# Moving the feed-forward pairs of a two-pass software pipeline: first pairs at their last possible step, the later second pairs one step earlier

## What is computed

```python
x = x + 0.5 * _L1_ffn_ref(_layernorm(x), w_gate, w_up, w_down)      # first feed-forward
x = x + _L1_attn_ref(_layernorm(x), in_proj_weight, ...)           # second attention
x = x + 0.5 * _L1_ffn_ref(_layernorm(x), w_gate, w_up, w_down)      # second feed-forward
...
def fp4_linear(x, w):                      # blocks of 16 along the last dim
    return einsum(fp4_quant_dequant(x), fp4_quant_dequant(w))
gate = fp4_linear(x, w_gate); y = fp4_linear(x, w_up)
return fp4_linear(silu(gate) * y, w_down)  # 128 -> 352 -> 128
```

## Time and profile before

| | |
|---|---|
| median of 3 runs | 1892.03 us (1891.06 to 1893.39) |
| the profiled execution | 1895.74 us, its span 1893.7 us |
| the tail within the span | from about 1177 us to 1893.7 us |
| busy over the whole span | PE 84%, DVE 66%, ACT 54%, POOL 37% |
| granted clock of TensorE, by stretch | 0.77 (1177 to 1285 us), 0.92 (1285 to 1554), 1.00 (1554 to 1735), 0.84 (1735 to 1821), 0.62 (1821 to 1894) |
| PE busy in the same stretches | 64.2 of 108 us, 227.0 of 269, 149.6 of 181, 57.5 of 86, 34.6 of 73 |

### The profile page before, as it was taken

How to read it: one execution, slowest core, us unless ns; L and a number is a source line. 1 busy time by engine, 2 the same in 40 slices (tenths; PEclk the granted TensorE clock), 3 DMA queues, 4 the chain that set the end, 5 groups by cost and what they waited for, 6 DMA issues and landing times. The chain is left out here.

```text
span 1893.7 us, 35220 instructions
## 1 busy us (share of the span) xinstructions
PE 1583.6 (84%) x12162; PEld 1091.9 (58%) x12167; DVE 1250.6 (66%) x2566; ACT 1020.1 (54%) x2035; POOL 707.3 (37%) x1144
## 2 busy tenths in 40 slices
PE   6999947999999999998899993576888898878654
PEld 5668835555555555554666782354666676666443
DVE  6635558888888788882753665686668777675333
ACT  2434423788888888885333441233556656655421
POOL 0787634011111111111088763432344554443530
PEclk9999978999999999999699996688899999999876
DMA  6123421111111111110512343000000000000000
GB/s 246 36 78 85 133 69 31 34 29 34 29 29 40 29 34 29 29 29 8 201 47 84 95 119 108 3 1 1 2 2 2 8 5 7 5 7 8 4 7 8
DMA packets 50494, 83.08 MB, mean 44 GB/s; under 512 B 11124, under 2 KB 35124, under 8 KB 49652
## 3 DMA queue, kind: packets, MB, share of 16 engines
q1 hardware_dynamic: 41236, 62.07, 11.4%
q0 software_dynamic: 9088, 18.76, 2.9%
HBM read 43.18 MB, written 31.22 MB: 39 GB/s over the span
## 5 line engine op out<-in xcount | busy, mean ns | idle before, releaser
L1883 DVE TENSOR_REDUCE z_parts<-z_pM 128x4 f32<-128x512 f32 x576 | 373.2, 685 | 95.3 <-PE z_pM L1621 91.4
L1798 ACT ACTIVATE z_Pr<-z_pE 128x512 f32<-128x512 f32 x576 | 322.5, 597 | 84.9 <-PE z_pE L1645 82.1
L1990 POOL TENSOR_SCALAR_AFFINE_SELECT z_Pr<-z_Pr 128x512 f32<-128x512 f32 x128 | 81.6, 637 | 480.6 <-ACT z_Pr L1798 480.6
L1645 PE MATMUL z_pE<-z_QM,z_QK 128*128 128x512 f32 x576 | 250.5, 437 | 8.0 <-DMA z_QM<-z_Q 5.5
L1621 PE MATMUL z_pM<-z_KM,z_Q 128*128 128x512 f32 x576 | 233.5, 410 | 1.5 <-DVE z_Q L1873 0.9
L1645 PEld LDWEIGHTS z_pE<-z_QM,z_QK 128*128 128x128 f32 x576 | 107.6, 188 | 158.9 <-ACT z_Pr L1798 91.4
L356 POOL DMA_INDIRECT slot_results<-m_yq,m_xq x156 | 152.4, 977 | 74.8 <-ACT m_yq L561 43.1
L332 POOL DMA_INDIRECT slot_rows<-m_XN,m_dest x128 | 130.0, 1016 | 94.8 <-DVE m_dest L650 59.4
L1658 PE MATMUL z_pO<-z_Pr,z_V 128*9 128x512 f32 (+3 forms) x1536 | 159.3, 488 | 0.1
L960 PE MATMUL f_gup<-s_wguT,f_xT 128*128 128x352 f32 x256 | 117.5, 545 | 41.8 <-DVE f_src L1240 31.6
L1109 ACT ACTIVATE f_sg<-f_gup 128x176 f32<-128x176 f32 x128 | 40.7, 318 | 162.2 <-PE f_gup L960 162.0
(11 more groups left out here) (274 smaller groups left out, 3888.9 us busy)
## 6 DMA issues: line engine op xcount, KB each, us to landing
slot_rows<-in_c_pad SPq DMA_DIRECT2D x2, 5070.0 KB, 24.4
m_xq<-slot_rows SPq DMA_DIRECT2D x38, 260.0 KB, 3.5
z_QM<-z_Q SPq DMA_DIRECT2D x128, 64.0 KB, 2.0
z_KM<-z_QK SPq DMA_DIRECT2D x60, 128.0 KB, 2.4
m_raw<-in_gu SPq DMA_DIRECT2D x2, 2048.0 KB, 8.7
m_XN<-slot_results SPq DMA_DIRECT2D x8, 512.0 KB, 4.2
m_raw<-slot_results SPq DMA_DIRECT2D x8, 512.0 KB, 5.9
slot_results<-m_yq,m_xq POOLq DMA_INDIRECT x156
```

Source lines behind the costliest of these rows:

```text
L1645: mm(pE[e % 2][:, :].rearrange("p (h c) -> p h c", h=4), QK[G % RING][:, kt * P:(kt + 1) * P], QM[half][:, :, q * P:(q + 1) * P], start=Tr ...
L1798: a.activation(Pr[j % 4][:, :, q * P:(q + 1) * P], pE[e % 2][:, :].rearrange("p (h c) -> p h c", h=4), ACT.Exp, scale=DH0 ** -0.5).then_in ...
L1883: v.tensor_reduce(parts[:, qt, kb, :], pM[n % 3][:, :].rearrange("p (h k) -> p h k", h=4), AX.X, ALU.max).then_inc(maxed, 1)
L1990: g_.affine_select(blk, blk, [[0, 4], [1, P]], ALU.is_ge, 0.0, base=0, channel_multiplier=-1).then_inc(selected, 1)
```

## The change

Two table entries change. The first passes, which stood at steps 0 to 6 without a gap and then at every second step to 24, stand at 0, 1, 2, 4, 6, ... 28. The second passes, at 17, 19, ... 47, stand at 17, 19, ... 29 for pairs 0 to 6 and at 30, 32, ... 46 for pairs 7 to 15. The last step of all goes from 50 to 49. No instruction is added or removed but those that go with a quantisation of other width; the attention and the statistics keep their ticks.

```diff
     AHEAD = 12
-    FIRST = {p: p if p < 6 else 6 + 2 * (p - 6) for p in range(NP2)}
-    SECOND = {p: 2 * p + 17 for p in range(NP2)}
+    FIRST = {p: max(p, 2 * p - 2) for p in range(NP2)}
+    SECOND = {p: 2 * p + (17 if 2 * p + 16 <= FIRST[NP2 - 1] else 16) for p in range(NP2)}
     PAIR = {n: (p, 0) for p, n in FIRST.items()} | {n: (p, 1) for p, n in SECOND.items()}
```

## The result

The changed kernel takes 1874.8 us (median of 4 runs, 1874.29 to 1876.98), the kernel before 1892.7 us (1891.06 to 1895.32): ratio 0.9906, 95% interval 0.9889 to 0.9924, 17.9 us less. Timed again, with five runs of the changed kernel against 17 of the one before, it was 0.9903 (0.9889 to 0.9918). The forecast was 8.9 us less. So the direction and most of the places were right, but the gain was twice the forecast: 1874.8 us is inside the range of the prediction (1873 to 1892), near its low end, and outside the 1877 to 1888 of the forecast alone. A gain of more than 17 us, which came, had been given a chance of 0.05.

A forecast was written before the change was run, and what follows sets the result against it. PE work was taken to bound the tail's middle and a chain of Q and G halves its end. Terms from -12.6 to +6.3 us summed to -8.9, giving 1883.1 us; range 1873 to 1892, forecast alone 1877 to 1888.

The forecast's parts named there:

- a string of halves: Each pair's Q half (quantisation start, DVE L1216, to transposes, PE L952) and G half (to next L1216) sum to the end.
- The crowded ticks: Ticks 52 to 59 carry a first and a second pass per step: +6.3 us; 52 to 63 over 105 us means wrong.
- the step to pair 8: From tick 60 to second pair 8's quantisation, which starts two ticks earlier: -12.6 us.
- The stretch from pair 9 to 11: Halves beside full attention, sized from first passes in ticks 26 to 33: 60.4 us against 58.9, +1.5; low bound 56.
- the early ticks: Ticks 8 to 17, where steps 3 and 5 lose first passes: -1 us, bounds -10 and +4.
- pair 11's Q half: Still has scores and softmax beside it, so 12.2 us; pair 11 to 12 changes by 0.
- The end behind pair 15: Behind the start of the last second pair nothing changes: 0.
- The Q halves of pairs 12 to 14: Quantisation halves after the projections end: 9.1 us each, bounds 7.0 and 12.2.
- POOL's block: `inverse_root` and `expand` ahead of `scale_back` hold up the Q half; moved behind, 12.2 us becomes 9.1 in three halves.
- Q halves would not get shorter: Rival: statistics, added projection and attention on DVE replace POOL's work; 12.2 us stays, +9.3, 1892.4 us; chance 0.19.
- the scale comes too late: Rival: ACT's `normalise` waits for `inverse_root`; 1903 us if that takes 14; chance 0.13, shared with other crowded-tick costs.
- the early part gains too: Rival: early ticks at -10 us and 28 us periods for pairs 9 to 11: 1871 us; over 17 us gained, chance 0.05.

The follow-up runs named there:

- the repeat: Both kernels profiled and timed again without an edit: spans 1891.6 us before and 1874.4 us changed, tails 711.7 and 693.3 us.
- POOL's order turned: Against the kernel before, old tables: `inverse_root` of second passes one tick later, behind `scale_back`; ratio 0.9886, tail 689.7 us.
- second table alone, statistics off the Q half: Against the kernel before: new second-pass table, old first-pass table, second-pass statistics on DVE behind the quantisation's seventh step; ratio 0.9866, tail 681.2 us.
- second table alone: Against the kernel before: only the second-pass table is new, first passes stay as they were; ratio 0.9894, tail 695.0 us.
- changed, statistics off the Q half: Against the changed kernel: second-pass statistics on DVE moved to the end of the odd tick, behind the seventh step; ratio to before 0.9840, tail 681.4 us.
- the longer `inverse_root`: Against the changed kernel: six iteration turns instead of three in `inverse_root` of second passes; ratio to before 0.9944, tail 703.8 us.
- the version one step further: Against the kernel before: all second passes at 2p + 15, `inverse_root` one tick behind the statistics; ratio 1.0103, tail 725.3 us.

## Why the prediction was right, and half the size

*The frame held.* That the tail's end is a string of halves, and that halves before can be put together to those after, gave every stretch of the table within 2.3 us (3.5 in the repeat). The crowded ticks cost 6.2 for 6.3, the step to pair 8 earned 13.2 for 12.6.

*Where the missing 7.5 us are* (16.4 in the mean of the tails for 8.9). No stretch carries them alone. The stretch from pair 9 to 11 was mis-sized most, by 2.1 us in this pair of profiles and 3.5 in the repeat. I had taken its halves from ticks 26 to 33, and named as their weakness that these ran partly at half clock, but took the value, not the bound. The windows agree with that: the granted clock is 0.89 in the rows of comparison (1358 to 1389 us) and 0.94 and 0.97 in the stretch itself, in the two profiles of the changed kernel. No run isolates it. With this stretch go the early ticks (2.3 too little) and pair 11's Q half (10.9 us, not 12.2). The end behind pair 15 was 1.3 us shorter here but only 0.2 in the repeat, so that is scatter. The Q halves of pairs 12 to 14 were 9.4, 9.4 and 8.0 for 9.1. That the time fell inside the range is in part luck: the terms behind the low end, -10 in the early ticks and 28 us for each period of pairs 9 to 11, came to -3.3 and to 29.2 (28.4 in the repeat), and they add up to about 1870, not to the 1871 given.

*What the experiments add to the ledger.* The tails, cut at the start of second pair 8, in us (two profiles where two numbers stand; one kernel's differ by up to 2 in a part):

| kernel | to the start of pair 8 | from there to the end |
|---|---|---|
| before | 479.6, 480.8 | 230.8, 230.9 |
| before, POOL's order turned | 476.8 | 212.9 |
| second table alone, statistics off the Q half | 463.8 | 217.4 |
| second table alone | 466.0 | 229.0 |
| changed | 470.5, 468.7 | 225.6, 224.7 |
| changed, statistics off the Q half | 466.0 | 215.4 |

Ahead of pair 8 the change earned 10.7 us (forecast 7.3), behind it 5.7 (forecast 1.6). The first is the shortened lag and the early ticks' gain, less what the crowded ticks cost, as the prediction booked it. The second is a small difference of two large parts, which the prediction did not see apart. POOL's order alone, in the old time line, is worth 18 us there. The statistics inside the Q half take 10 to 12 back. The prediction gave POOL's block its price in three halves only, 3.1 us each after all that takes its place, and the statistics 1.2 in each of them; for pairs 8 to 11 its rows of comparison hold both effects unseen. So it did not find that each of the two can be had, or left out, by itself. No run moves the tables and leaves `inverse_root` ahead of `scale_back`, so what the shift alone is worth behind pair 8 stays open.

*The signs.* PE's idle time before L952 of pair 12 fell from 6.85 to 4.13 us, L1383 starts right behind L1231 (1774.77, next fence, and 1773.48 + 1.16), and the crowded ticks 52 to 63 took 101.5 us, under 105. One sign of being wrong appeared: the early part ends at 1276.88 us, not within 2 of 1285.4. Of these 8.6 us, 6.2 are the scatter ahead of the tail, from which marks that count from the start of the span can't be told apart; the other 2.4 are the gain of the early ticks, which had been put at 1.

*POOL's block got shorter beside a G half.* POOL's `inverse_root` for the pair after took from 1777.71 to 1782.15 us, 4.4 us for 7.7 before:

```profile
1774.77 0.62 POOL L1383 TENSOR_TENSOR f_q<-f_y,f_neg 128x256 f32<-128x256 f32 x1 [3.98 <-issue]
...
1777.71 0.21 POOL L1358 TENSOR_SCALAR f_var<-f_var 128x2 f32<-128x2 f32 x1
...
1778.58 0.19 POOL L1362 TENSOR_TENSOR f_sq<-f_sq,f_var 128x2 f32<-128x2 f32 x1
...
1781.97 0.22 POOL L1369 TENSOR_SCALAR f_shift<-f_sq 128x2 f32<-128x2 f32 x1
1782.15 1.05 POOL L1407 TENSOR_TENSOR f_pm<-f_Pn,k_mask 128x512 f32<-128x512 f32 x1
...
1791.73 0.48 ACT L1096 ACTIVATE f_src<-k_X,f_shift,f_rstd 128x128 f32<-128x128 f32 x1
```

It now lies beside a G half, in which DVE multiplies out of PSUM, and no L1362 from 1735 us on takes more than 0.2 us. The prediction had expected less than 7.7 by a rule of the Trainium skill, SBUF — State Buffer, section "Who interferes with whom", and the trace agrees. The 3.3 us are a part of the scale's slack: here it is ready 9.5 us before ACT's `normalise` starts, and 4.9 to 10.1 for pairs 8 to 15, where the prediction reckoned with 2.2 and 4.6.

*The rivals.* That Q halves would not get shorter is refuted by their 9.4, 9.4 and 8.0 us, though its mechanism is there: behind pair 8 the statistics gave back some 10 us of the gain. That the scale comes too late is refuted for this change by the longer `inverse_root` and confirmed by the version one step further. That the early part gains too came to a third of its bound, while the shorter periods of pairs 9 to 11 nearly came in full.

One difference between runs goes with the clock. The second table with the old first one spent 3 to 4 us more between pairs 8 and 11 than with the new one (93.7 against 90.9 and 89.5 us). The granted clock there is 0.93 against 0.96 and 0.98, and PE is busy 80.2 us against 77.4 and 76.0 with the same 1130 matmuls, which is all of the difference. Why the clock was lower stays open.

## What to carry to other kernels

In a pipeline written by hand, look not only at which engine is busy but at what stands in front of the hand-over in its neighbour's queue. Here 16 small instructions on an engine busy 37% of the time cost 18 us or more, and one line that puts them behind the hand-over earned about as much as the shift of the whole time line (0.9886 and 0.9906; by the tails, more). When a shift takes work out of one queue's critical half, ask into which half the other engines' work falls instead; here that was the statistics, and moving them off as well was a separate edit worth some 13 us more. Shortening the lag by one step gained; shortening it until the scale was due in the tick in which it is made cost 47 us in the crowded ticks, 36 of them spent waiting for it. Making the side work longer on purpose, and looking where the time comes back, tells how much slack a pair still has.

## What the runs showed of the hardware

The stages ahead of the tail, with the same instructions, ended between 1177 and 1183 us in nine profiles, and at 1211 to 1216 in the three from another chip, while the tail's marks agreed within 2 us up to tick 30: compare a part by its own first and last row, not by the span. DVE's L1225 took 1.89 us beside POOL's `expand` in the Q halves of pairs 11 and 12, before the change as after it, and 1.16 us in those of pairs 14 and 15, where no `expand` stands beside it. DVE's L1227 took 0.64 us before the change, in the Q half of pair 12:

```profile
1785.90 0.64 DVE L1227 TENSOR_SCALAR f_m<-f_y 128x960 uint32<-128x960 uint32 x1
```

After it, with a second `expand` moved up into the place of `inverse_root`, it took 1.31 us (1769.99, above). So 0.7 us of the 2.4 by which this Q half exceeds pair 15's 7.0 are a price of the very move that shortened it.
